# Attention probabilities turned by VectorE blocks and a trip through device memory instead of by TensorE

## The reference

```
xn  = layernorm(x)                                   # no affine part
a   = attention(xn): qkv = xn @ W_qkv, 16 heads of 64, rotary q and k,
      scores = q k^T / 8, causal mask, softmax, times v, then @ W_out
f   = a block with its own attention of 16 heads of 8 (not causal) and @ Wo,
      x2 = xn + layernorm(that) * g1 + be1,
      8 experts: gate softmax, the top 2 of them weighted and summed,
      f = x2 + layernorm(moe) * g2 + be2
out = x + a + f
```

## Time and profile before

| | |
|---|---|
| median of 3 runs | 1234.73 us (1233.05 to 1240.54) |
| the profiled execution, as timed | 1231.06 us |
| its span, first to last instruction | 1229.2 us |
| mean granted TensorE clock | 0.986 of full |
| busy: TensorE / VectorE / ScalarE / GpSimd | 1119.0 / 895.1 / 859.3 / 813.1 us |
| bytes moved by DMA | 55.46 MB, 45 GB/s over the span |

### The profile page before, as it was taken

The page is one execution under the profiler, slowest core; times in us unless marked ns, Lnnn a source line. Parts: engine busy times, 40 slices in busy tenths (PEclk is TensorE's granted clock), DMA queues, the critical chain, the costliest instruction groups (busy, mean ns, idle before and its releaser), DMA issues.

```text
span 1229.2 us, 25101 instructions
## 1 busy us (share of the span) xinstructions
PE 1119.0 (91%) x9242; PEld 718.3 (58%) x9242; DVE 895.1 (73%) x2275; ACT 859.3 (70%) x1793; POOL 813.1 (66%) x728
## 2 busy tenths in 40 slices
PE   3789999989899998989999899899989999899997
PEld 2465566556565565745657566565566556575565
DVE  6667487875768767787677966788487866878557
ACT  2478776587756877568775787758876687757871
POOL 3485875586756767657675688657695668576760
PEclk9999999999899999989999999999999999999998
DMA  5211201021111120111110111001111011111100
GB/s 161 60 35 36 65 35 32 18 79 43 40 31 39 57 60 32 32 49 48 57 39 18 56 59 57 23 35 48 49 57 31 29 54 41 48 40 39 49 14 10
DMA packets 40934, 55.46 MB, mean 45 GB/s; under 512 B 7398, under 2 KB 18920, under 8 KB 40812
## 3 DMA queue, kind: packets, MB, share of 16 engines
q1 hardware_dynamic: 37340, 50.90, 13.3%
q10 hardware_dynamic: 3472, 2.95, 0.8%
HBM read 5.60 MB, written 2.10 MB: 6 GB/s over the span
## 4 chain that ended last, share of the span: by engine, by line
PE 64%; DVE 17%; ACT 10%; issue 4%; POOL 2%; DMA 1%; SPq 1%; ACTq 1%; DVEq 0%; POOLq 0%
PE work L1707 9%; PE work L1734 8%; PE work L1722 8%; DVE fnmax L1467 7%; PE work L1629 6%; PE work L1784 6%; PE work L1631 5%; PE work L1630 5%; PE work L1750 4%; ACT fpt L1298 4%; PE work L1759 4%; PE work L1774 3%; ACT pn L1340 3%; DVE work L1589 2%; PE work L1742 2%
## 5 line engine op out<-in xcount | busy, mean ns | idle before, releaser
L1467 DVE TENSOR_REDUCE fnmax<-work 128x2 f32<-128x1024 f32 x256 | 301.9, 1218 | 68.4 <-PE work L1759 67.9
L1201 POOL TENSOR_TENSOR raw<-raw,cos_t 128x512 f32<-128x512 f32 x128 | 164.1, 1282 | 251.5 <-DMA swapped<-raw 233.9
L1340 ACT ACTIVATE pn<-work,nmax 128x512 f32<-128x512 f32 (+3 forms) x512 | 264.5, 533 | 89.3 <-DVE nmax L1589 86.8
L1298 ACT ACTIVATE fpt<-work 128x1024 f32<-128x1024 f32 x256 | 252.6, 1029 | 65.1 <-PE work L1774 58.9
L1589 DVE CUSTOM_DVE_ANT_0 work<-work,causal 128x512 f32<-128x512 f32 (+3 forms) x512 | 236.3, 519 | 81.1 <-PE work L1707 80.9
L1722 PE MATMUL work<-consts,pn 128*128 128x128 f32 x1280 | 173.1, 279 | 6.6 <-DVE fnmax L1467 3.5
L1205 POOL TENSOR_TENSOR raw<-raw,swapped 128x512 f32<-128x512 f32 x128 | 163.8, 1280 | 10.0
L1722 PEld LDWEIGHTS work<-consts,pn 128*128 128x128 f32 x1280 | 143.4, 142 | 40.4 <-DVE fnmax L1467 8.3
L1202 POOL TENSOR_TENSOR swapped<-swapped,sin_t 128x512 f32<-128x512 f32 x128 | 166.0, 1297 | 0.0
L1216 POOL TENSOR_TENSOR qk_l<-raw,qk_h 128x512 fp32r<-128x512 f32 x128 | 162.9, 1280 | 2.7
L1352 ACT COPY pt<-work 128x1024 f32<-128x1024 f32 x128 | 129.2, 1020 | 36.8 <-PE work L1722 36.2
(11 more groups left out here) (155 smaller groups left out, 1939.8 us busy)
## 6 DMA issues: line engine op xcount, KB each, us to landing
swapped<-raw SPq DMA_DIRECT2D x256, 128.0 KB, 2.0
fqs<-fqn SPq DMA_DIRECT2D x96, 128.0 KB, 2.7
x_in<-in_L_attn_x_dram SPq DMA_DIRECT2D x8, 256.0 KB, 4.2
out_dram<-x_in SPq DMA_DIRECT2D x7, 256.0 KB, 2.5
fpt<-in_L_attn_W_qkv_dram ACTq DMA_DIRECT2D x3, 512.0 KB, 6.0
pt<-in_L_ffn_We_dram ACTq DMA_DIRECT2D x1, 512.0 KB, 9.6
wout<-in_L_attn_W_out_dram ACTq DMA_DIRECT2D x1, 512.0 KB, 12.4
out_dram<-x_in SPq DMA_DIRECT2D x2, 128.0 KB, 1.8
```

The lines of the kernel that those rows point to most:

```text
L1201: nc.gpsimd.tensor_tensor(raw[:, n % 3], raw[:, n % 3], cos_t[:], ALU.mult)
L1298: nc.scalar.activation(fpt[:, ((b * G + g) * T + i) % FP, 2 * r:2 * r + 2].rearrange("p h n -> p (h n)"), bank_of(("fst", b, g, i), 2 * r, 2),
L1340: ins = nc.scalar.activation(pn[:, h, PN_AT[j]:PN_AT[j] + n], bank_of(("sc", b, c, unit), h)[:, at:at + n], ACT.Exp, scale=-1.0, bias=nmax ...
L1467: nc.vector.tensor_reduce(fnmax[:, j, 2 * r:2 * r + 2, 0:1], bank_of(("fsm", b, g, j), 2 * r, 2).rearrange("p (f n) -> p f n", f=2), AX.X, ...
```

## The change

Steps `tp`, `tq`, `tpe`, `tqe`, `fan`, `rT` and `rb` go. In their place:

- `exp` writes `pn` in another layout: columns are gathered by their remainder by four, so that each 32x32 block of VectorE's transpose holds keys 4r + a of a query block. `pn` now has two buffers in two parts (2048 and 512 floats in each partition), `pt` has only one.
- `tr` (VectorE, three for each stage, 1024, 1024 and 512 elements in each partition) transposes the 32x32 blocks in place.
- `put` and `put2` (SyncE) write the two parts to device memory (1 MB and 256 KB); `get` and `get2` read them back with partitions regrouped, in runs of 2 KB and 512 bytes. `get` of a stage waits for `put` of the same stage to land and for `pv` of the stage before.
- `inv` also transposes the reciprocals; `lput` writes them to device memory and `lget` (two DMAs) reads them back spread over 64 partitions each. `div` waits for that.
- `pv` has seven groups of four strips in place of four: three over 256 columns and four over 128, the moving data in runs of 32 floats.
- `xn`, `nm1` and `nm2` move to ScalarE, as an activation with scale and bias; VectorE's statistics get one small instruction more (the negated mean), GpSimd's `rs` steps one small product more.
- Some start-up data lie in other buffers, and `PLACE` and `PSUM` are written anew for all steps. On SyncE's queue a stage then reads, in batch 3: `put 3, put2 3, get2 3, get 3, lput 3, swap (6,0), lget 3, put 4, swap (6,1), put2 4, lput 4, get 4, swap (7,0), get2 4, lget 4`. On TensorE `pv` of a stage stands about one and a half stages behind its `sc`; the steps that make q and k keep their distance to `sc`.

```diff
-    "PE": (..., "proj", "v", "sc", "tp",
-           "tq", "pv", "rT", "ao"),
+    "PE": (..., "proj", "v", "sc", "pv", "ao"),
-    "ACT": (..., "raw", "vc", "exp", "tpe", "fan", "rb"),
+    "ACT": (..., "raw", "vc", "xn", "nm1", "nm2", "exp"),
-    "DVE": (..., "max", "tqe", "inv", "div", "yadd"),
+    "DVE": (..., "max", "tr", "inv", "div", "yadd"),
-    "SP": ("swap", "fdup", "store", "load"),
+    "SP": ("swap", "put", "get", "put2", "get2", "lput", "lget", "fdup", "store", "load"),
...
-        pn = sb("pn", [P, 2, PT_N])
-        pt = sb("pt", [P, 2, 2, PT_N])
+        pn = [sb(f"pn{n}", [P, 2, QUADS, 2, tiles, STRIP]) for n, tiles in enumerate(PT_N)]
+        pt = [sb(f"pt{n}", [P, QUADS, 2, tiles, STRIP]) for n, tiles in enumerate(PT_N)]
...
+                elif kind in ("put", "put2"):
+                    c, part = x_[2], int(kind == "put2")
+                    wait(sp, after("tr", b, c, 1 + part))
+                    wait(sp, landed("get" + kind[3:], *ring(2, b, c, NC)))
+                    sp.dma_start(turned[part][c % 2], pn[part][:, c % 2].rearrange("p c h n r -> p (c h n r)")).then_inc(put_done[part][c % 2], 16)
+                elif kind in ("get", "get2"):
+                    c, part = x_[2], int(kind == "get2")
+                    wait(sp, landed("put" + kind[3:], b, c))
+                    wait(sp, after("pv", *ring(1, b, c, NC)))
+                    sp.dma_start(pt[part][:].rearrange("p a h n r -> p a (h n r)"),
+                                 turned[part][c % 2].rearrange("(a s) (c n) -> (s c) a n", a=QUADS, c=QUADS)).then_inc(get_done[part][c % 2], 16)
+                elif kind == "lput":
+                    wait(sp, after("inv", b, c))
+                    wait(sp, landed("lget", *ring(2, b, c, NC)))
+                    sp.dma_start(l_turned[c % 2].rearrange("c (a r) -> a c r", a=QUADS), l_inv[:]).then_inc(lput_done[c % 2], 16)
+                elif kind == "lget":
+                    wait(sp, landed("lput", b, c))
+                    wait(sp, after("div", *ring(1, b, c, NC)))
+                    for h in range(2):
+                        sp.dma_start(l_wide[h * DH:(h + 1) * DH], l_turned[c % 2, h * T:(h + 1) * T].rearrange("(a c) n -> a (c n)", a=1)
+                                     .broadcast_to([DH, S])).then_inc(lget_done[c % 2], 16)
...
+            def normalise(kind, n, dst, src):          # on ScalarE
+                for t in range(T):
+                    ins = nc.scalar.activation(dst(t), src(t), ACT.Identity, scale=rstd[:, n, t:t + 1], bias=shift[:, n, t:t + 1])
...
-                        wait(act, after("tp", *ring(1, b, c, NC), 1))
-                        wait(act, after("tq", *ring(1, b, c, NC)))
+                        wait(act, landed("put", *ring(2, b, c, NC)))
+                        wait(act, landed("put2", *ring(2, b, c, NC)))
...
+                elif kind == "tr":
+                    c, unit = x_[2:]
+                    wait(dve, after("exp", b, c, unit, 0), after("exp", b, c, unit, 1))
+                    part, tiles = UNIT_AT[unit]
+                    blocks = pn[part][:, c % 2, :, :, tiles].rearrange("p c h n r -> p c h (n r)")
+                    nc.vector.transpose(blocks, blocks).then_inc(done["tr"], 1)
...
-                    nc.vector.reciprocal(l_inv[:], l_sum[:, c % 2]).then_inc(done["inv"], 1)
+                    nc.vector.reciprocal(l_inv[:, 0:2 * T], l_sum[:, c % 2].rearrange("p h t -> p (h t)")).then_inc(dve_link, 1)
+                    dve.wait_ge(dve_link, link())
+                    nc.vector.transpose(l_inv[:], l_inv[:]).then_inc(done["inv"], 1)
...
-                    wait(pe, after("tpe", b, c, 0), after("tpe", b, c, 1))
-                    wait(pe, after("tqe", b, c))
+                    wait(pe, landed("get", b, c))
+                    wait(pe, landed("get2", b, c))
...
-                    for i in range(T):
+                    for i, js in ((0, (3, 2)), (0, (0,)), (0, (1,)), (1, (3, 2)), (1, (1,)), (2, (3, 2)), (3, (3,))):
```

More of the change, by code:

```diff
@@ new lines @@
+    "proj": [
[8 rows of a table added]
+    ],
+    "tb": [
+        [3],
+    ],
+    "fqk": [
+        [2],
+        [84],
+        [203],
+        [324],
+        [445],
+        [566],
+        [687],
+        [808],
+    ],
+    "fv": [
+        [11],
+        [120],
+        [234],
+        [354],
+        [479],
+        [599],
+        [719],
+        [848],
+    ],
+    "fsm": [
[8 rows of a table added]
+    ],
+    "fmT": [
+        [13, 29, 56, 81],
+        [122, 139, 177, 202],
+        [244, 266, 297, 323],
+        [361, 387, 417, 444],
+        [484, 508, 542, 565],
+        [604, 629, 660, 686],
+        [727, 747, 784, 807],
+        [849, 873, 905, 926],
+    ],
@@ new lines @@
+    "ao": [
+        [97, 155],
+        [218, 276],
+        [340, 397],
+        [462, 518],
+        [583, 639],
+        [704, 760],
+        [825, 881],
+        [943, 969],
+    ],
+    "cT": [
+        [127],
+        [248],
+        [369],
+        [490],
+        [611],
+        [732],
+        [853],
+        [954],
+    ],
+    "wo": [
+        [131],
+        [252],
+        [374],
+        [494],
+        [615],
+        [736],
+        [860],
+        [956],
+    ],
+    "x2T": [
+        [145],
+        [265],
+        [386],
+        [507],
+        [626],
+        [750],
+        [870],
+        [961],
+    ],
@@ new lines @@
+    "gate": [
+        [149],
+        [270],
+        [391],
+        [512],
+        [633],
+        [754],
+        [875],
+        [962],
+    ],
+    "moe": [
+        [156, 160, 161, 163],
+        [277, 281, 282, 284],
+        [398, 402, 403, 405],
+        [519, 523, 524, 526],
+        [640, 644, 645, 647],
+        [761, 765, 766, 768],
+        [882, 886, 887, 889],
+        [963, 965, 966, 967],
+    ],
+    "smh": [
+        [4],
+    ],
+    "wh": [
+        [1, 3, 7],
+    ],
+    "xn": [
+        [0],
+        [30],
+        [162],
+        [283],
+        [401],
+        [501],
+        [611],
+        [740],
@@ L426 @@
     ],
     "ch": [
[L428 to L435 removed]
+        [124],
+        [237],
+        [350],
+        [463],
+        [576],
+        [689],
+        [802],
+        [894],
+    ],
+    "nm1": [
+        [129],
+        [245],
+        [355],
+        [469],
+        [581],
+        [695],
+        [809],
+        [900],
     ],
     "x2h": [
[L438 to L441 removed]
@@ L903 @@
         KEYS[kind] = [(half,) for half in range(2)]
-    elif kind in ("div", "fan", "inv", "pv", "rT", "rb", "tq", "tqe"):
+    elif kind in ("div", "inv", "lput", "lget", "pv", "put", "get", "put2", "get2"):
         KEYS[kind] = [(c,) for c in range(NC)]
@@ L1062, in build @@
         fdup_done = [sem(f"fdup{n}_done") for n in range(2)]
+        put_done = [[sem(f"put{part}_{n}_done") for n in range(2)] for part in range(2)]
+        lput_done = [sem(f"lput{n}_done") for n in range(2)]
+        lget_done = [sem(f"lget{n}_done") for n in range(2)]
+        get_done = [[sem(f"get{part}_{n}_done") for n in range(2)] for part in range(2)]
         x_loaded = [sem(f"x{n}_loaded") for n in range(XB)]
@@ L1293, in _ @@
                     if b == 0:
+                        wait(act, after("tt", 0))
                         for n in range(3):
@@ L1737, in _ @@
+                            ins = nc.tensor.matmul(psum[a:a + STRIP, at:at + len(js) * P], v[:, i, 2 * c + h, a % DH:a % DH + STRIP],
+                                                   moving.rearrange("p a j r -> p j a r"),
+                                                   start=(i, js[0]) == (0, 3), stop=i == T - 1, tile_position=(0, a), skip_group_check=True)
                     ins.then_inc(done["pv"], 1)
-                elif kind == "rT":
-                    c = x_[2]
-                    wait(pe, after("fan", b, c))
-                    for t in range(T):
-                        ins = nc.tensor.transpose(psum[:, tile(t)], l_wide[:, tile(t)], ident)
-                    ins.then_inc(done["rT"], 1)
```

963 lines of the change are left out of this document (407 added, 556 removed), and 478 rows, old and new, of tables (PLACE, PSUM).

## The result

| | before | changed |
|---|---|---|
| median | 1237.63 us (4 runs) | 1291.00 us (4 runs, 1287.86 to 1296.19) |
| ratio | | 1.0431, 95% interval 1.0366 to 1.0497 |
| profiled execution, its span | 1231.06, 1229.2 us | 1288.85, 1287.1 us |
| mean granted TensorE clock | 0.986 | 0.892 |
| forecast | | 1171 (1100 to 1280) |

A forecast was written before the change was run, and what follows sets the result against it. VectorE was taken as the new bound: 125.6 us a batch at 92% busy gives 136.5 for 146.4. Seven periods save 69 us, the end adds 5: span 1165, median 1171 us, range 1100 to 1280.

The forecast's parts named there:

- Rivals 1 and 3: VectorE and GpSimd hindering each other, 1215 to 1250 us, chance 0.12; VectorE's transposes far below one element a cycle, 1345, 0.07.
- The rule of the Trainium skill: For kernel authors: transpose 128x128 on TensorE where PSUM will do as destination, leaving VectorE blocks of 32x32.
- The DMA trip ... Hidden, as long as SyncE issues in time.: `put` then `get`, 10 to 11 us, hidden because `pv` stands about 25 us behind its scores.
- I take 92%.: VectorE's busy share of a batch period: 125.6 us of work gives 136.5 us a batch.
- It is the new bound: VectorE, at 125.6 us a batch, bounds the changed kernel, by 14 us over TensorE.
- That warning: The prediction is wrong above all if VectorE falls well under 90% busy; every point is 1.5 us a batch.
- Rival 2: SyncE's queue delays the swaps that GpSimd waits for: 1274 us with 2 us each, range 1225 to 1330, chance 0.20.
- its tipping point of 1.1: Mean delay in us of each swap from which GpSimd decides the time, in a period of 136.5 us.

The follow-up runs named there:

- the small trip: The changed kernel with `put`, `put2`, `get` and `get2` moving 32 KB each in place of 1 MB or 256 KB: 1207.33 us for 1291.00.

## Why the prediction was wrong

**Right: the engines' costs.** VectorE was forecast at about 1025 us and has 1007.0. TensorE: 1119.0 - 214.2 + 12.8 = 918 us were forecast. By the estimate used above (half of the 235 us, and of the 28 before, that it was busy at the lower level of its clock) its work at full speed is 1037.2 - 117.5 = 920 us for 1119.0 - 14 = 1105 before: 185 us of the 201 forecast as gone did go. `pv`'s seven groups, priced at 13 us, were free. The transposes cost 1.23, 0.70 and 0.21 us. `put` landed in 4.6 us for the 5.1, both legs in the 10.5 of "10 to 11". Rivals 1 and 3 fell with that: the transposes keep within 665 to 1248 ns, and GpSimd's products stay at 1281. The rule of the Trainium skill that stood against the change (VectorE: DVE Perf Modes, rules for kernel authors) would have had the right side, but the traces do not bear out a high price of VectorE's transposes as such: 155 us less of them gave 16.

**Wrong, the first failing step: "The DMA trip ... Hidden, as long as SyncE issues in time."** It was compared with the 25 us between `sc` and `pv` as one sum of two landings. What the trace has between the end of `exp` and the start of `div` is 21.5 us in the mean, for 17.4 before, and each part of that way has an engine's order behind it: `put` waits for the last transpose, `get` for `put`, `pv` for `get` and for its turn, `lput` and `lget` for the queue. The bytes of the two legs carry 84 us of the time, most of it (69) by the way back. Such traffic without anybody waiting costs 17 in the kernel before; that the rest is waiting follows from the difference and from the waits in the traces, not from a run that changes the waits alone. The prediction priced the reciprocals' trip at no time on the path. Leaving it out gives 31 us as the kernel stands, and nothing with the trip small: what it costs, it costs behind the 1.25 MB of `get`.

**Wrong, the second: "I take 92%."** It was borrowed from TensorE's share in a kernel whose order was another. VectorE reached 79.6%, and 84.5 with the small trip. "It is the new bound" falls with it: 155 us less of its work gave 16, and 6 with the small trip. By the prediction's own scale (1.5 us a batch for each point) 92 for 80% is 18 us a batch, and the period is 155.2 for 136.5. With the small trip it is 1207, 36 over the forecast: the period, (975.7 - 105.4) / 6 = 145.1 us by the starts of its batches, is still 8.6 too long, 51 us in six periods, and the start-up before batch 1, which the forecast left as it was, is 11 us shorter than before (105.4 for 116.7). So the utilisation was wrong beside the trip too, and the start-up hides a part of that by luck. That warning stood in the prediction's last paragraph, but with no chance and no place in the range.

**Missed altogether: the clock.** All terms were taken at 0.986. In the changed kernel TensorE stands still more (19% of the span for 9), the granted clock is 0.892, and what it still has to do gets longer: of the 119 us between the forecast busy time and the measured 1037.2, 117.5 - 14 = 103 are the lower clock. The estimate holds together: it gives 915 to 921 us of work for every variant of the changed kernel that leaves TensorE's work as it is, while their busy times go from 1012 to 1077. How much of the 103 reaches the end was not isolated. Filling the gaps raised the clock and lost time; taking `pv` work away lowered it and half of the gain was gone.

**Rival 2 had the right side and, by accident, the right size.** Its signs are in the trace: GpSimd's wait for swaps grew from 233.9 to 290.7 us, and swaps go out 2.1 us later than before, over its tipping point of 1.1. Yet two kernels with prompter swaps (0.14 and 0.85 us) are slower, and one with swaps as late (2.37) is 69 us faster. A sign that came with the slow kernel was not the cause of these 84 us.

**The normalisations**, priced at nothing on the path, cost 20 us in the order of before, and 28 to 38 when they are moved back in that of the changed kernel. Every edit that moved steps without a new plan of the whole cost time, 20 to 162 us, whichever way it went. So the single price of that move in a plan made for it stays open. Open too is what makes up the last 36 us with the small trip: without most of VectorE's transposes it was 6 less, within what single runs scatter; TensorE's lower clock, the swaps, which go out 2.1 us after `raw` there too, and the new order as such were not separated. That a second `pt` would let `get` start earlier was not tried, nor was a second queue for the reciprocals.

## What to carry to other kernels

Work that leaves a full engine for a DMA round trip did not become free here: where every engine waits in line, count the trip from the producer's last instruction to the consumer's first, with every queue place between, a small transfer right behind a megabyte among them, and not by landing times against one distance. Where several engines have 75 to 85%, don't take a full one as the bound: removing 155 us of VectorE's work gave 16 here, and shortening one transfer that others wait for gave 69.

## What the runs showed of the hardware

- VectorE's float32 transpose of 32x32 blocks, on 128 partitions within SBUF, takes 1235 ns for 1024 elements in a partition, 697 for 512 and 211 for 32, and didn't get longer beside a GpSimd that is 63% busy (at most 1248).
- A DMA of 16 KB took 5.6 us to land when issued 0.6 us behind 1.25 MB on the same queue, and 2.0 at another time. 1 MB landed in 4.6 us on the way out and 5.9 on the way back (medians, from issue). The Trainium skill (DMA: Bandwidth & Descriptors, section Bandwidth) has 6.15 us of the DMAs' busy time for 1 MB from HBM to SBUF, issued from GpSimd; on the way back this comes near it, on the way out it is less.
- Some 180 GB/s of DMA traffic that nobody waits for cost this kernel 1.4%; the swaps' median landing went from 2.0 to 2.1 us, and their longest from 3.8 to 8.8.
- TensorE's clock stood at 0.50 from 573 to 576 us, in which it was busy 3 us of 3, right behind two stretches of 3 us in which it had been busy 1.03 and 1.65. At 0.50 the same instruction took 422 ns for 273.
